# One step of a transformer kernel: the wait of a projection, and the place of moments and inverse deviations in two queues

## What is computed

```python
x = x + attn(layernorm(x), wq, wk, wv, wo)       # K, V, Q = 64 wide, energy = K^T V
x = x + ffn(layernorm(x), W_fc, W_proj)          # no softmax: context = Q @ energy

def attn(x):
    Q, K, V = x @ wq.T, x @ wk.T, x @ wv.T
    energy = einsum('bnd,bne->bde', K, V)        # sum over a batch's 1024 tokens
    return (Q @ energy) * sqrt(3 / 64) @ wo.T
def ffn(x):
    h = square(relu(x @ W_fc.T))                 # 1024 wide
    y = h @ W_proj.T
    return spike_count(y) / 5                    # 5 steps of an integrate-and-fire neuron
```

## Time and profile before

| | |
|---|---|
| median of 3 runs | 473.5 us (472.54 to 473.52) |
| the profiled execution | 470.9 us |
| its span on the core | 469.1 us |
| TensorE busy | 455.9 us, 97% of the span |
| VectorE, ScalarE, GpSimd busy | 358.3, 281.7, 239.5 us |
| granted TensorE clock | full throughout, 0.997 on average |

### The profile page before, as it was taken

How to read it: one execution, slowest core, us unless ns; L and a number is a source line. 1 busy time by engine, 2 the same in 40 slices (tenths; PEclk the granted TensorE clock), 3 DMA queues, 4 the chain that set the end, 5 groups by cost and what they waited for, 6 DMA issues and landing times. The chain is left out here.

```text
span 469.1 us, 8195 instructions
## 1 busy us (share of the span) xinstructions
PE 455.9 (97%) x2844; PEld 402.6 (86%) x2844; DVE 358.3 (76%) x922; ACT 281.7 (60%) x521; POOL 239.5 (51%) x196
## 2 busy tenths in 40 slices
PE   8998999999999999999999999999999999999993
PEld 7576788998888899898889989898988989898993
DVE  4767677878878787887878788786878885868667
ACT  3559657566475756657575665757665565656530
POOL 2028465645657554655655465565546553434430
PEclk9999999999999999999999999999999999999998
DMA  8514025252523525252352425244232404040111
GB/s 304 133 45 92 0 46 129 69 135 58 152 46 91 133 66 134 65 144 45 91 136 73 129 69 136 46 120 106 74 86 67 92 1 128 8 125 12 45 46 45
DMA packets 120969, 41.29 MB, mean 88 GB/s; under 512 B 114016, under 2 KB 114656, under 8 KB 120672
## 3 DMA queue, kind: packets, MB, share of 16 engines
q1 hardware_dynamic: 120928, 40.78, 33.9%
HBM read 25.03 MB, written 15.73 MB: 87 GB/s over the span
## 5 line engine op out<-in xcount | busy, mean ns | idle before, releaser
L398 POOL TENSOR_TENSOR hid_l<-hid,hid_h 128x512 fp32r<-128x512 f32 x128 | 166.4, 1303 | 181.9 <-ACT hid_h L452 181.9
L442 ACT ACTIVATE relu<-hid_ps 128x512 f32<-128x512 f32 x128 | 76.3, 596 | 118.4 <-PE hid_ps L893 117.3
L891 PE MATMUL y_ps<-wdn_h,hid_h 128*128 128x256 f32 x480 | 136.2, 284 | 0.1
L893 PE MATMUL y_ps<-wdn_h,hid_l 128*128 128x256 f32 x480 | 135.8, 283 | 0.0
L892 PE MATMUL y_ps<-wdn_l,hid_h 128*128 128x256 f32 x480 | 135.8, 283 | 0.0
L891 PE MATMUL hid_ps<-x2T_h,wup_h 128*128 128x512 f32 x256 | 105.6, 413 | 0.8 <-DVE x2T_l L705 0.8
L892 PE MATMUL hid_ps<-x2T_l,wup_h 128*128 128x512 f32 x256 | 100.9, 394 | 0.0
L893 PE MATMUL hid_ps<-x2T_h,wup_l 128*128 128x512 f32 x256 | 100.0, 391 | 0.0
L891 PEld LDWEIGHTS y_ps<-wdn_h,hid_h 128*128 128x128 f32 x480 | 91.5, 191 | 9.6 <-POOL hid_l L398 5.1
L774 DVE SCALAR_TENSOR_TENSOR cnt<-y_ps,bound,cnt 128x256 f32<-128x256 f32 x240 | 98.6, 474 | 0.2
L892 PEld LDWEIGHTS y_ps<-wdn_l,hid_h 128*128 128x128 f32 x480 | 91.6, 191 | 4.2
(11 more groups left out here) (151 smaller groups left out, 574.1 us busy)
## 6 DMA issues: line engine op xcount, KB each, us to landing
xs<-x_dram SPq DMA_DIRECT2D x15, 512.0 KB, 4.6
out_dram<-x SPq DMA_DIRECT2D x15, 512.0 KB, 2.6
x_blocks<-x SPq DMA_DIRECT2D x56, 128.0 KB, 2.7
x_block<-x_blocks SPq DMA_DIRECT2D x14, 512.0 KB, 3.7
x_block<-x_dram SPq DMA_DIRECT2D x104, 64.0 KB, 2.6
hid<-w_up_dram SPq DMA_DIRECT2D x1, 1024.0 KB, 7.9
x<-w_down_dram SPq DMA_DIRECT2D x1, 1024.0 KB, 10.0
xs<-x_dram SPq DMA_DIRECT2D x2, 256.0 KB, 4.1
```

The source lines that it names most:

```text
L398: nc.gpsimd.tensor_tensor(hid_l[:, i % 2, c, :], hid[:, c % 4, :], hid_h[:, i % 2, c, :].bitcast(f32), ALU.subtract).then_inc(hid_ready, 1)
L442: nc.scalar.activation(relu[:, c % 2, :], hid_ps[c % 2][:, :], ACT.Relu).then_inc(relu_done, 1)
L891: mm(dst, a[0], b[0], start=start, stop=False)
L893: return mm(dst, a[1], b[0], start=False, stop=stop)
```

## The change

It touches only the order of four pieces of work and one wait; no instruction is added or removed.

- TensorE: `project_kv` waits for `kv_in_scale` of the group before, not for its `kv_ready`.
- GpSimd: the inverse deviation of group 2 goes from behind `hid_l` of chunk 0 to between the two halves of `wdn_l`; that of group 3 goes from in front of chunk 6 to in front of chunk 4.
- VectorE, step 0: the moments of x of group 3 go from behind `kv_low_half(0, 2)` to behind `residual(0, 1)`; the moments of x1 of group 1 go from the end to in front of `kv_scale(0, 3)`.

```diff
@@ GpSimd, step @@
-                    if is_first(r, i) and c in (1, 6):
-                        inverse_deviation(r, 2 if c == 1 else 3)
+                    if is_first(r, i) and c == 4:
+                        inverse_deviation(r, 3)
@@ GpSimd, before the steps @@
             low_half_of_weights(wdn_high, wdn_raw, wdn_h, wdn_l, wdn_ready, 0)
+            inverse_deviation(0, 2)
             low_half_of_weights(wdn_high, wdn_raw, wdn_h, wdn_l, wdn_ready, 1)
@@ VectorE, first_step @@
                 residual(0, 1)
+                first_moments(0, 3)
                 q_low_half(0, 2)
                 kv_scale(0, 2)
                 kv_low_half(0, 2)
-                first_moments(0, 3)
                 x2T_low_half(0, 1)
+                moments(0, 1)
                 kv_scale(0, 3)
                 kv_low_half(0, 3)
-                moments(0, 1)
@@ TensorE, project_kv @@
                 if there(r, n - 2):
-                    pe.wait_ge(kv_ready, upto(r, n))
+                    pe.wait_ge(kv_in_scale, n)
```

## The result

The changed kernel takes 471.6 us in the median of 11 runs (469.7 to 474.7), the kernel before 473.5 (472.5 to 477.0, now 11 runs). The ratio is 0.9947, 95% interval [0.9926, 0.9968]: 1.5 to 3.5 us less. Forecast were 472.4 and 1.1 us less (0.9977). The median lies in the range. By the ratio the gain is 2.5 us, more than twice the forecast; between the two medians it is 1.9.

What follows compares the result with a forecast made beforehand. TensorE was taken to bound the kernel, with idle time to win only around step 0: 1.32 (first stall) + 0.39 (third) = 1.71, less 0.65 for kv_scale(0,2), 1.1 us less: 472.4 us from 473.5; range 471.1 to 473.4.

Steps and rivals of the forecast that it cites:

- What bounds the kernel: TensorE, busy 381.34 of 381.40 us from 58.6 to 440; only a few idle us around the first step can be won.
- The three stalls: TensorE waits in step 0: k and v of group 3 (1.76 us), its energy sum (0.66), energy times wo (0.39).
- The wait of project_kv: TensorE, k and v of group 3: waiting for kv_scale(0,2) starts them 1.68 us earlier if kv_scale stands still.
- kvT late next: TensorE then waits for ScalarE's kvT of group 3: 0.36 us given back, 1.32 left.
- The second stall stays: Energy sum of group 3: its wait hangs on TensorE's chunk 7 through ScalarE, so it moves but keeps its length.
- moments(0,1) ahead of kv_scale(0,3) is covered: VectorE, step 0: kv_scale ends by 50.3 at most, ScalarE asks at 51.0, so 0.7 us of cover.
- The third stall goes: Energy times wo of group 3: q follows the low half of k and v at once, winning 0.39 us.
- Does kv_scale(0,2) stand still?: VectorE, step 0: no, collisions with GpSimd make it 0.65 us late, which counts in full against the 1.71.
- the first hold: GpSimd's inverse deviation of group 2 holds VectorE's second xT_l from 36.6 to 37.35; it ends 0.84 us late.
- A: Rival for step 0: no collision of GpSimd and VectorE, the 1.71 us stay whole or nearly, 471.8 us; chance 0.34.
- D: Rival for the steady rounds: later waits take the gain back, within 0.2 of 473.5 us; chance 0.12.

Runs made afterwards that it cites:

- the gate: One wait added to the kernel before: GpSimd's low half of k and v starts only after VectorE's pair of x<-cnt,x; 471.1 us beside 473.96.
- wait_rest: Kernel before with project_kv's new wait only from group 4 on; 474.42 us, the kernel before beside it 474.91.
- wait_rest_again: wait_rest measured once more on another chip; 472.20 us, ratio 1.0 to the kernel before.
- gate_wait: Kernel before with the gate and project_kv's wait alone changed, both queues as before; 470.0 us.
- gate_kvhigh: Changed kernel with the gate and ScalarE's high half of k and v of group 3 ahead of hid_h of chunk 7; 469.06 us.
- gate_stay_kvhigh: gate_kvhigh with moments of x of group 3 and inverse deviation of group 2 in their old places, that of group 3 ahead of hid_l 5; 469.85 us.
- after_again: The changed kernel measured once more, 12 runs; median 469.99 us.
- wait_3: Kernel before with project_kv's new wait for group 3 alone; 472.05 us, the kernel before beside it 474.91.

## Why the prediction was wrong

- *What bounds the kernel.* The three stalls, their releasers and the statement that only step 0 has idle time were read rightly from the profile, but of one execution. **This is the step that failed**: "that stretch can only be shifted, not shortened". The profiled execution had lost no tie; an execution of median length takes 2 to 3 us more, and the gate, which acts in just that stretch, takes them away (471.1 beside 473.96); in two profiles with the same step 0 (wait_rest, wait_rest_again) five and three costly ties are lost there. The sign was in plain view: 470.9 us against runs of 472.54 and up. I moved the gain from the one to the other and never asked what the 2.6 us between them were. The change then got its further 0.7 us (by the medians) to 1.3 (by the ratio) from fewer lost ties, which nothing in the prediction foresaw.
- *The wait of project_kv*: 1.68 us at kv_ps if kv_scale stands still. gate_wait confirms it: k and v of group 3 start 13.90 us behind the first up-projection matmul, where they start 15.59 behind it before.
- *kvT late next*, 0.36 us given back: TensorE waits for it, 0.19 after, 0.15 in gate_wait.
- *The second stall stays* and hangs on ScalarE's order: right, and gate_kvhigh wins its 0.83.
- *moments(0,1) ahead of kv_scale(0,3) is covered*: right, kv_scale(0,3) ends at 50.17 and ScalarE begins with it at 51.49. gate_stay_kvhigh shows what it costs without the cover.
- *The third stall goes*: right.
- *Does kv_scale(0,2) stand still?* 0.65 us late in the forecast, 0.33 measured. The direction of the first hold was wrong: GpSimd's inverse deviation waited for VectorE's xT_l, not xT_l for it, though it had started 0.4 us before the second of them wanted to: recorded starts didn't tell who would hold whom. The 0.75 us of the hold (36.6 to 37.35) had no row behind it. The price that came was line 670's meeting with GpSimd, 0.30 (the hid_l of 39.92 takes 1.30 and ends at 41.22, line 670 at 41.24). So the sum of step 0 came near the measured one with a hold in it that never took place, which is luck in part. Step 0 gave 1.39 us in the profile and 1.2 between the gated medians, where the sum had 1.06.
- *The rivals.* A (no collision, 1.7) and the forecast lie on either side of step 0's 1.2 to 1.4. D looked for a wait in the steady rounds that would eat the gain; there was one, but its losses grew fewer. That the rounds could win anything was on no list, though the rows at 404.95 and 405.20, which show VectorE losing a meeting of the same kind, were among mine, used for a price alone.
- Had the tie been lost as often after as before, 1.2 to 1.4 us would have been the result, at the edge of what a measurement tells.

## What to carry to other kernels

Before a profiled execution is made the base of a sum, compare its time with every run of the same kernel: if it lies outside them, find what differs first. Look in each steady round for two engines that ask for the same thing within a few hundredths of a microsecond; such a tie makes scatter, and an edit ahead of it can change the median by more than its own worth. A wait that settles the order (here one line on GpSimd, 471.1 against 473.96) takes most of the scatter away and makes later edits of a few tenths measurable.

After an edit that lengthens a stall of TensorE, look at the granted clock behind it, run by run: moves that were worth nothing in the sum cost 1.6 us more in some executions.

## What the runs showed that I had not expected

- A tie whose recorded starts differ by no more than 0.02 us between its two outcomes decides over 1.1 us of VectorE. GpSimd's low half of k and v takes 1.30 alone, 1.85 when the pair goes first and 1.52 when it goes between the two.
- 16 idle transpositions put in at 45 us, which cost TensorE 1.7 us where they stand (30.73 against 29.00 at energy times wo), raised the median by 2.8 (477.22 against 474.41 side by side); the rest falls in the rounds behind.
- Whether an execution loses much or nothing seems to be settled in part for the whole of it: of after_again's twelve runs nine are at the loss-free time and three 3 to 4.5 us above; before beside wait_3 has five at 471.6 to 472.3 and six at 474.9 to 476.2. What settles it is open.
